# One more TensorE product ahead of each tile's wait, in the message stages of a two-layer graph network

## The reference

```
e     = leaky_relu(a_src[src] + a_dst[dst], 0.2)
m     = segment_max(e, dst);  p = exp(e - m[dst])
denom = segment_sum(p, dst)
out   = segment_sum((p / denom[dst]) * h[src], dst)
```

## Time and profile before

| what | value |
|---|---|
| median of 3 runs | 10629.55 us |
| lowest and highest run | 10615.75, 10659.98 us |
| span of the profiled execution | 10639.3 us |
| first and last sum of stage g0sm (L1352) | 668.6 and 3229.7 us |
| first and last sum of stage g1sm (L1352) | 5810.8 and 8440.8 us |
| PE, DVE, ACT, POOL busy over the span | 69%, 58%, 32%, 49% |
| mean granted TensorE clock over the span | 0.805 |

### The profile page before, as it was taken

How to read it: one execution, slowest core, us unless ns; L and a number is a source line. 1 busy time by engine, 2 the same in 40 slices (tenths; PEclk the granted TensorE clock), 3 DMA queues, 4 the chain that set the end, 5 groups by cost and what they waited for, 6 DMA issues and landing times. The chain is left out here.

```text
span 10639.3 us, 84665 instructions
## 1 busy us (share of the span) xinstructions
PE 7303.5 (69%) x22541; PEld 4282.3 (40%) x22541; DVE 6218.5 (58%) x17557; ACT 3449.0 (32%) x7448; POOL 5204.1 (49%) x5326
## 2 busy tenths in 40 slices
PE   1536555665668999998775656556666548999965
PEld 0412222232234555554444223323233245666644
DVE  8956666666666555554324767777777752332334
ACT  0323333333333333332224333333333352232223
POOL 0146666666661000002334666666666466666652
PEclk9757777777779999999987766676767659999987
DMA  3156566666651000001225655556566542222237
GB/s 104 62 158 194 186 190 189 189 187 190 188 187 54 25 24 24 24 22 27 22 14 177 191 177 188 184 184 190 184 190 195 163 121 49 64 61 60 66 105 234
DMA packets 665409, 1341.19 MB, mean 126 GB/s; under 512 B 202523, under 2 KB 401278, under 8 KB 664034
## 3 DMA queue, kind: packets, MB, share of 16 engines
q0 software_dynamic: 238688, 579.40, 21.4%
q1 hardware_dynamic: 399616, 730.71, 19.8%
q10 hardware_dynamic: 26626, 25.65, 0.7%
HBM read 711.27 MB, written 636.81 MB: 127 GB/s over the span
## 5 line engine op out<-in xcount | busy, mean ns | idle before, releaser
L1352 PE MATMUL g1sm_sump<-g_acc,g1sm_to 128*128 128x264 f32 x3520 | 1546.0, 555 | 1009.0 <-DVE g_acc L1498 495.6
L1352 PE MATMUL g0sm_sump<-g_acc,g0sm_to 128*128 128x260 f32 x3520 | 1497.8, 539 | 1014.8 <-DVE g_acc L1498 437.2
L1245 POOL DMA_INDIRECT g_acc<-htab,g1sm_src x1760 | 1733.5, 985 | 927.3 <-issue 583.9
L1245 POOL DMA_INDIRECT g_acc<-htab,g0sm_src x1760 | 1714.3, 974 | 901.6 <-issue 543.4
L1498 DVE TENSOR_TENSOR g_acc<-g_acc 128x256 f32<-128x256 f32 x3520 | 1470.1, 418 | 405.1 <-remote 95.5
L1352 PEld LDWEIGHTS g1sm_sump<-g_acc,g1sm_to 128*128 128x128 f32 x3520 | 719.0, 248 | 1781.3 <-issue 1073.5
L1352 PEld LDWEIGHTS g0sm_sump<-g_acc,g0sm_to 128*128 128x128 f32 x3520 | 697.0, 242 | 1761.0 <-issue 1091.7
L798 POOL DMA_INDIRECT re_rerows<-rtab,re_resrc x1024 | 994.5, 971 | 524.6 <-issue 285.3
L2376 DVE SCALAR_TENSOR_TENSOR g_acc<-f_yp,f_wgt,g_acc 128x256 f32<-128x256 f32 x784 | 342.9, 479 | 1132.3 <-PE f_yp L2296 933.0
L1521 DVE SCALAR_TENSOR_TENSOR g_acc<-g_acc,g0sm_side,g0sm_sump 128x260 f32<-128x260 f32 x1705 | 815.5, 478 | 296.0 <-remote 147.3
L1521 DVE SCALAR_TENSOR_TENSOR g_acc<-g_acc,g1sm_side,g1sm_sump 128x264 f32<-128x264 f32 x1705 | 822.5, 482 | 121.1 <-PE g1sm_sump L1352 53.4
(11 more groups left out here) (453 smaller groups left out, 9121.7 us busy)
## 6 DMA issues: line engine op xcount, KB each, us to landing
sums<-g_acc SPq DMA_DIRECT2D x440, 528.0 KB
sums<-g_acc SPq DMA_DIRECT2D x440, 520.0 KB
z<-k_arena SPq DMA_DIRECT2D x96, 512.0 KB
k_arena<-z SPq DMA_DIRECT2D x33, 1024.0 KB
g_acc<-htab,g0sm_src POOLq DMA_INDIRECT x1760
g_acc<-htab,g1sm_src POOLq DMA_INDIRECT x1760
x<-g_acc POOLq DMA_DIRECT2D x48, 512.0 KB, 3.4
re_rerows<-rtab,re_resrc POOLq DMA_INDIRECT x1024
```

Of the source, the lines that this page charges most:

```text
L1245: nc.gpsimd.indirect_dma_start(slot[a][:, u, :], None, table, bass.IndirectOffsetOnAxis(ap=src[a][:, u:u + 1], axis=0)).then_inc(landed[a] ...
L1352: nc.tensor.matmul(sump[u % BANKS][:, 0:W], to[u // LOT % RING][:, u % LOT, :], slot[a][:, u, 0:W], start=True, stop=True).then_inc(summed, 1)
```

## The change

In `add_up` one more product stands between the wait for the lot's matrix and the wait for the message. Its operands are the constants `ident` and `ones`, both 128 x 128 and in 32-bit floats; it writes 128 columns of a PSUM bank that nobody reads, and counts no semaphore. The bank comes free because `firstp` and `fixp`, which had a bank each, now share one. `add_up` runs once for each tile, so there are 1760 more products in each of the two stages.

```
--- before.py
+++ after.py
@@ -1182,7 +1182,8 @@
         asrc = c.sb("asrc", [P, 2 * H, T])
         fix = c.sb("fix", [1, H])
         sump = [c.ps(f"sump{j}", [P, 512]) for j in range(BANKS)]
-        inp, backp, firstp, fixp = (c.ps(n, [P, 512]) for n in ("inp", "backp", "firstp", "fixp"))
+        inp, backp, smallp, spare = (c.ps(n, [P, 512]) for n in ("inp", "backp", "smallp", "spare"))
+        firstp, fixp = smallp[:, 0:G * P], smallp[:, G * P:G * P + H]
@@ -1348,6 +1349,7 @@
                 def add_up(a, k, u):
                     if u % LOT == 0:
                         pe.wait_ge(to_ready, k * LOTS + u // LOT + 1)
+                    nc.tensor.matmul(spare[:, 0:P], K["ident"][:, :], K["ones"][:, :], start=True, stop=True)
                     pe.wait_ge(msg_ready, k * T + u + 1)
                     nc.tensor.matmul(sump[u % BANKS][:, 0:W], to[u // LOT % RING][:, u % LOT, :], slot[a][:, u, 0:W],
                                      start=True, stop=True).then_inc(summed, 1)
```

## The result

The changed kernel takes 10686.7 us (median of 5 runs, 10678.33 to 10689.83) against 10629.55 us (5 runs, 10615.75 to 10659.98).

A forecast was written before the change was run, and what follows sets the result against it. It took the bound to be a loop of POOL, transfers, DVE and PE, POOL's own work 86% of the time. Cost +50 less gain 20 gave +30 us; shifted to the runs' median, 10660 us; 8-in-10 range 10520 to 10790.

The forecast's parts named there:

- The likeliest case: Whole kernel: clock rises to about 0.80, time +30 us to 10660, own range 10600 to 10700; 0.43 with C and D.
- the price of 50 us: Message stages: 40% of 77 us for starts at 1.2 GHz plus 47 us for block turns gets through.
- 0.7 us reaches DVE: Plain halves starting at 1.2 GHz: PE falls 2.0 us behind, 1.3 to spare; 110 starts, 77 us, bounds 0 and 220.
- At 2.4 GHz: cost nothing: Message tiles: PE is asked for 0.71 us a tile, under DVE's 0.86, the product running while PE waits for the message.
- The turn, 47 us: Turn of a block at 1.2 GHz: transposes wait 0.86 us longer in half of 110 turns; bounds 0 and 143 us.
- The gain of 20 us ahead of adds: DVE's waits ahead of L1521: higher clock shortens sums by 0.56 us, a sixth of 114 us; bounds 0 and 114.
- rival B: Message stages: PE's queue bounds every start at 1.2 GHz, POOL waits for later sums; +145 us, 10775 us; chance 0.33.
- POOL's idle time takes up the difference: Message stages: POOL's idle beyond 0.30 us a gather, 374 and 399 us, must take up the whole time difference.
- The slow stretches should be as many and as long: Message stages: stretches of 3.5 us a tile stay unchanged; otherwise the loop settled differently and the sum is wrong.
- A: Rival, message stages: faster by the clock, which shortens most waits ahead of L1521; -114 us, 10520 us; chance 0.24.
- C: Rival: nothing moves, clock stays and products fit PE's idle time; 10630 us; 0.43 shared with the forecast and D.
- D: Rival: the product's constants raise no clock level, cost without gain; 10680 us; 0.43 shared with the forecast and C.

The follow-up runs named there:

- the repeat: The changed kernel measured again, against the kernel before at 10637.12 us: 10680.23 us, ratio 1.0037 (1.0022 to 1.0051).
- two products: Two added products a tile instead of one, against the kernel before at 10637.12 us: 10795.51 us, ratio 1.0145 (1.0127 to 1.0164).
- POOL's finer waits: Kernel before, no added product, POOL waiting for one tile's sum ahead of each gather, not four ahead of four; against it at 9537.1 us: 1.0000 (0.9991 to 1.0009).

## Why the prediction was right or wrong

**Sign and size.** Forecast +30 us, measured +57 (+43 in the repeat): same side, inside the range, the size forecast a half to seven tenths of what came. The likeliest case (the clock rises, the time does not follow, some tens of us are paid) is what came. The steps behind the number fare worse: the price of 50 us was put on PE being full at 1.2 GHz, and the waits that grew are not waits for PE's work.

**The clock: right.** 0.80 was forecast for both windows. By the Trainium skill ("TensorE: Matmul & The Clock Gate", section "Terms": penalty about throttled time times 1 - K/N) the fall of the half-clock share from 54 to 40% and from 58 to 34% is an estimate of (0.14 x 2561 + 0.24 x 2630) / 2 = 495 us to be gained. The runs disagree: 57 us were lost, and 43 us in the repeat.

**The prices: right.** Timeline of PE in the changed kernel, at the start of a plain half (L1354 a sum, L1352 an added product):

```profile
1414.40 1.23 PE L1354 MATMUL g0sm_sump<-g_acc,g0sm_to 128*128 128x260 f32 x2 [7.28 <-DVE g_acc L1500]
1415.42 0.63 PE L1352 MATMUL g0sm_spare<-k_ones,k_ident 128*128 128x128 f32 x2
1415.85 1.07 PE L1354 MATMUL g0sm_sump<-g_acc,g0sm_to 128*128 128x260 f32 x2
...
1417.14 1.07 PE L1354 MATMUL g0sm_sump<-g_acc,g0sm_to 128*128 128x260 f32 x2
...
1419.75 0.60 PE L1354 MATMUL g0sm_sump<-g_acc,g0sm_to 128*128 128x260 f32 x2
...
1420.41 0.60 PE L1354 MATMUL g0sm_sump<-g_acc,g0sm_to 128*128 128x260 f32 x2
```

At 1.2 GHz sums start 1.45 and 1.29 us apart (1.32 forecast), at 2.4 GHz, from 1418.4 on, 0.66 us (0.71 forecast).

**"0.7 us reaches DVE" at each start at 1.2 GHz, 77 us: wrong, it is at its lower bound.** Timeline of DVE at the same place:

```profile
1405.65 0.42 DVE L1500 TENSOR_TENSOR g_acc<-g_acc 128x256 f32<-128x256 f32 x1
1412.87 0.49 DVE L1509 SCALAR_TENSOR_TENSOR g0sm_carried<-g0sm_smallp,g_acc 128x256 f32<-128x256 f32 x2 [6.79 <-DMA sk_x<-x]
...
1414.77 0.43 DVE L1500 TENSOR_TENSOR g_acc<-g_acc 128x256 f32<-128x256 f32 x1
1415.11 0.48 DVE L1523 SCALAR_TENSOR_TENSOR g_acc<-g_acc,g0sm_side,g0sm_sump 128x260 f32<-128x260 f32 x1
1415.63 0.42 DVE L1500 TENSOR_TENSOR g_acc<-g_acc 128x256 f32<-128x256 f32 x1
```

DVE goes on in steps of 0.86 us with no wait ahead of its adds; the clock rises before the three steps of lead are used. Nor does it happen elsewhere: of the 406 waits ahead of adds in both stages, only one (0.2 us) ended less than 1 us after the sum that the add needs; in the repeat 11 of 408 did, 3 us in all. A sum that is late because PE is full would be taken at once. In all, DVE's waits ahead of adds that ended at 1.2 GHz fell from 336 us (170 waits) to 317 (168).

**"At 2.4 GHz: cost nothing": the step that failed.** Waits ahead of adds that ended at 2.4 GHz rose from 86 us (64 waits) to 340 (238), and to 616 with two products; part of that can be that the clock is at 2.4 GHz for more of the time. I had compared throughput, 0.71 against 0.86 us, and that holds; these waits are not PE's throughput. Timelines of PE and DVE in the second stage:

```profile
7172.39 0.61 PE L1354 MATMUL g1sm_sump<-g_acc,g1sm_to 128*128 128x264 f32 x2
...
7173.06 0.61 PE L1354 MATMUL g1sm_sump<-g_acc,g1sm_to 128*128 128x264 f32 x2
...
7173.73 0.66 PE L1354 MATMUL g1sm_sump<-g_acc,g1sm_to 128*128 128x264 f32 x2
...
7175.26 0.71 PE L1354 MATMUL g1sm_sump<-g_acc,g1sm_to 128*128 128x264 f32 x2 [0.65 <-issue]
```

```profile
7174.78 0.42 DVE L1500 TENSOR_TENSOR g_acc<-g_acc 128x256 f32<-128x256 f32 x1
7177.12 0.49 DVE L1523 SCALAR_TENSOR_TENSOR g_acc<-g_acc,g1sm_side,g1sm_sump 128x264 f32<-128x264 f32 x1 [1.91 <-PE g1sm_sump L1354]
```

The message of 7174.78 is summed at 7175.26. The add at 7177.12 stands right behind that message, so by LEAD = 3 it needs the sum three tiles before, that of 7172.39. That sum is over at 7173.00, and DVE takes it up 4.1 us later, after 1.91 us of idling. Pairing each add with its own sum in this way over both stages, the sum had been over for 4.9 us in the median wait of the changed kernel (6.5 us before, 4.3 us with two products, where 63 of 510 waits, 27 us in all, ended within 1 us). There the lead of three steps, 2.6 us, is used up, whatever the clock. It is not the store that every fourth add waits for as well: those adds have 205 of the 657 us.

Such late releases are no matter of PE alone. In the kernel before, in the slow stretch of the earlier trace rows, DVE waits for a result of its own:

```profile
1513.03 0.21 DVE L1474 SCALAR_TENSOR_TENSOR g0sm_fixc<-g0sm_cin,g0sm_ends,g0sm_ad 128x1 f32<-128x1 f32 x1
...
1517.02 0.43 DVE L1478 SCALAR_TENSOR_TENSOR g0sm_score<-g0sm_score 128x256 f32<-128x256 f32 x1 [1.28 <-DMA reach<-el_none]
```

L1478 waits for the count `weighed`, which only DVE raises, the last time with L1474. That was over at 1513.24, and L1478 starts 3.8 us later, after 1.28 us of idling (the name behind the arrow is one of the wrong ones). Waits of this kind, for DVE's own counts, took 352 us in the kernel before (319 waits), 11 us in the changed kernel (17 in the repeat) and none with two products. PE's late starts went with them: sums (the first of a lot left out) that start over 0.3 us late although message and PE are ready cost 274 us before, 22 us with the product and none with two. So the product did not leave the lateness as it was. It all but vanished where DVE waits for itself and where PE waits for DVE, and grew where DVE waits for PE, and the second outweighed the first. Why is not shown; no run separates it.

**The turn, 47 us: wrong.** The transposes were to come 0.86 us later in half of the blocks. From the end of the weights (L1484, in the changed kernel L1486) to PE's transpose it was 2.66 us in the mean of the 110 blocks before and is 1.90 us in the changed kernel (1.88 in the repeat, 2.16 with two products); to ACT's exponential 3.76 and 3.67 us. So PE's queue made nothing later there. The waits ahead of the first add of a block grew by 119 us, but the instance above is a late release: PE finished the correction at 1405.4 us (L1346 in the trace), and DVE took it at 1412.87, after 6.79 us of idling. That is no queue of PE.

**The gain of 20 us ahead of adds: wrong in place.** There waits grew. By the rows of the prediction, which had 341 us in 188 waits, they are 174.5 + 124.2 + 142.3 + 142.0 = 583 us, which was the sign of rival B. (Those rows leave out waits under other names; in all there were 234 of 422 us before.) They fell ahead of messages (-170 us) and of weight pieces (-120 us), which I had not priced.

**POOL's idle time takes up the difference: right,** 33 of 41 us, and 131 of 159 with two products.

**"The slow stretches should be as many and as long": wrong,** and with it the assumption that carries the sum. Stretches in which at least two messages running come 2 to 6 us after the one before went from 135 (1235 us in all) to 102 (676 us), while single pauses over 6 us went from 62 (631 us) to 104 (947 us). The loop did settle otherwise, by more than any term of the sum. The terms of +50 and -20 us are both not what the runs show, so that the forecast came near is luck.

**The rivals.** A fell to the repeat and to two products. B has the sign of the adds' waits right and its reason wrong: POOL's waits that end within 1 us of the sum it needs, as they would behind a full PE, were 89 before and 83 in the changed kernel (265 and 90 us), while those that end over 2 us after it rose from 145 to 243 (364 and 567 us); its price of 145 us was two and a half to three times too high. C is excluded by both intervals. D is refuted by the clock.

**What stays open.** What makes the releases late, why this occurs in some measurements only, why the added product shifts it from one pair of engines to another, and which half of the tiles carries the cost there: all runs of single halves, of the turn and of POOL's finer waits came on chips without slow stretches. So the cost is shown to come with the products and to lie in late releases of PE's results; its cause is not shown.

## What to carry to other kernels

A low clock is worth nothing to mend while the loop's step is the same at either level: here DVE's step was 0.86 us at both, and 0.05 to 0.08 more of clock over the span came with 43 to 158 us more of time. A sum of throughputs (0.71 us of PE under 0.86 us of DVE) did not bound the cost of work put into idle time: where releases arrive late, the slack that looks idle may already be spent, and two products cost more than twice what one cost. Before blaming an engine for a wait, pair the waiting instruction with the one that it needs by the program's order: the profile names the engine, but here the sum had been over for 4.9 us in the median wait. Run a change on more than one chip before explaining half a per cent: here the whole change costs 0.4 to 0.5% where releases arrive late, and on the faster chips neither half of it nor the doubled product in one half could be seen (the whole change was not run there).

## What the runs showed of the hardware that was not expected

The same program took 9537 to 9539 us on three chips and 10630 to 10637 us in the other measurements, 11% apart; 660 us of that lie in the two message stages, where in the slower measurements engines resume 2 us to over 10 us after the end of what they wait for (DVE at 1412.87 us for a correction of 1405.4), and even an engine that waits for its own earlier result does (3.8 us at 1517.02). On the faster chips the traces show no such wait. A gather is 0.94 to 0.95 us long in most rows, and its mean in the second stage was 984 ns with the idle product of PE behind the wait for the message and 1001 ns on the same chip with two of them ahead of it in half of the tiles; the shorter gathers came with 25 us less for the whole kernel.
